# First attention of a two-layer adaLN kernel: negated scores, one product as the division, weight casts on ScalarE, a new order on four engines

## The chip, the cores and the metric

The kernel runs on one core of a Trainium2 chip. Five engines work side by side, each through its own list in order: TensorE (PE; its weight loads are PEld), VectorE (DVE), ScalarE (ACT), GpSimd (POOL) and SyncE (SP), which issues the DMAs. They wait for each other on semaphores. The metric is the device time of one execution in microseconds (us).

## The reference, cut to what matters

Two layers on x of shape (2, 512, 512), each an attention block and a feed-forward block behind an adaptive layer norm. All is float32. The change touches only the first layer's attention:

```python
q = (x @ wq).reshape(B, S, 32, 128)     # 32 query heads, 8 key/value heads
k = (x @ wk).reshape(B, S, 8, 128)
v = (x @ wv).reshape(B, S, 8, 128)
q, k = _rope(q, pos), _rope(k, pos)
scores = jnp.einsum('bqhgd,bshd->bhgqs', qg, k) * sm_scale   # 128 ** -0.5
allowed = (j <= i) & (j > i - 128)
attn = jax.nn.softmax(jnp.where(allowed, scores, neg), axis=-1)
out = jnp.einsum('bhgqs,bshd->bqhgd', attn, v).reshape(B, S, 32 * 128)
return out @ wo                          # then x = x + ga * out
```

## The kernel before, in words

Float32 products are made of three matmuls (`mm3`): each operand is split into a rounded high part (written as float32r by a copy) and a low remainder (operand minus high part), and high x high, high x low and low x high are added in PSUM.

The first attention goes over 8 key/value heads (`kv_head(n, last)`: head 0 by itself, heads 1 to 6 in a hardware loop, head 7 with `last`). A head has two halves, one for each batch element b, numbered half = 2n + b. A half has four slots, one for each block of 128 queries (qb = 0 to 3), numbered slot = 4 half + qb. In a slot four query heads are done together: `scores` into banks 0 and 1; `mask` on DVE (L1126), which scales, adds the window, and keeps each row's maximum, then L1138 negates the four maxima; `exps` on ACT (L812), with the row sums beside them; `normalise` on DVE (L1140), a reciprocal of 128x4 and four multiplications (L1147); `transposes` on PE (L1568); `weights_high` on ACT and `weights_low` on DVE (the split); `sum_values` on PE into bank 4; `out_high` and `out_low` (the split of its result); `project_out` on PE into bank 5; `gate_attention` on DVE; `add_attention` on POOL into x. A query sees only its own and the preceding block of keys, so slot 0 of a half is 128 wide and the others 256.

Between these stand the projections of the next half (`project`: Q0 to Q3, Vt, which is V's transpose) and of the one after it (K, V), into banks 6 and 7 by turns. `evacuate` on DVE (three instructions, L1122 to L1124) makes the rope terms, POOL adds them (L613), ACT rounds (L806), POOL makes the remainder (L616). The weights of head n + 1 are split within head n: `split_weights` and `split_wo` cast on DVE (L1100, L1105), POOL subtracts (L602, L606). SP reloads a staging tile when `w_split` and `wo_split` say that it was read.

There is no planner: the order on each engine is the order in which the lines of that engine's `kv_head` stand. Buffers are few. `probs` and `nmax` have two copies, by qb % 2; banks 0 to 5, `pT_hi`, `oT_hi` and `gated` one. `scores(slot)` waits until slot - 1 is masked, `transposes(slot)` until slot is divided and `pT_lo` of slot - 1 is made, `sum_values(slot)` until `oT_lo` of slot - 1 is made, `project_out(slot)` until slot - 1 is gated.

Of the kernel before, what the change touches and what calls it, by code (L numbers as in the profile page):

```python
# [55 lines left out]
def adaln_two_layers(nc, a, out):  # L56
# [7 lines left out]
    with ctx:  # L64
# [51 lines left out]
        rmax = sb0("rmax", [P, 2, GQ])  # L116
# [166 lines left out]
        scores0, rowmax0, masked0, exp0, rden0, probs0 = (sem(n) for n in ("scores0", "rowmax0", "masked0", "exp0", "rden0", "probs0"))  # L283
# [312 lines left out]
        def _(pool):  # L596
# [11 lines left out]
            def rope(half, name, b):  # L608

                r = 5 * half + ROPE_NO[name]  # L610
                i = (b + ROPE_NO[name]) % 2
                pool.wait_ge(proj_free, TURNS * half + TURN[name] + 1)
                pool.tensor_tensor(rope_a[:, i], rope_a[:, i], rope_b[:, i], ALU.add).then_inc(rope_sum, 1)  # L613
                pool.wait_ge(rope_hi, r + 1)
                hi, lo = (kT_hi[:, b], kT_lo[:, b]) if name == "K" else (qT_hi[b][:, ROPE_NO[name] - 1], qT_lo[b][:, ROPE_NO[name] - 1])
                pool.tensor_tensor(lo, rope_a[:, i], hi.bitcast(F32), ALU.subtract).then_inc(rope_split, 1)  # L616

# [142 lines left out]
        def _(act):  # L760
# [51 lines left out]
            def exps(slot, qb):  # L812
# [3 lines left out]
                for h in range(GQ):  # L816
                    e = act.activation(probs[:, i, h, c], probs[:, i, h, c], ACT.Exp, bias=nmax[:, i, h:h + 1], scale=1.0,  # L817
# [8 lines left out]

            def kv_head(n, last):
                for b in range(B):
                    half, slot, nb = 2 * n + b, 8 * n + 4 * b, 1 - b
                    more = not (last and b == 1)  # L830
                    weights_high(slot, 0)
                    exps(slot + 1, 1)
                    if isinstance(n, int) and n == 0 and b == 0:
                        gates(0, 0, gate_a0)
                    out_high(slot)
                    if more:
                        rope_high(half + 1, "Q0", nb)
                    weights_high(slot + 1, 1)
                    if more:
                        v_high(half + 1, nb)  # L840
                        rope_high(half + 1, "Q1", nb)
                    exps(slot + 2, 2)
                    out_high(slot + 1)
                    weights_high(slot + 2, 2)
                    if more:
                        rope_high(half + 1, "Q2", nb)
                    exps(slot + 3, 3)
                    out_high(slot + 2)
                    if more:
                        rope_high(half + 1, "Q3", nb)  # L850
                    weights_high(slot + 3, 3)
                    if not last:
                        rope_high(half + 2, "K", b)
                    out_high(slot + 3)
                    if more:
                        exps(slot + 4, 0)

# [160 lines left out]
        def _(dve):  # L1018
# [70 lines left out]
            def split_weights(n, tiles):  # L1089

                for m in tiles:
                    src = st_kv[:, m] if m < 2 else st_q[:, :, (m - 2) * HD:(m - 1) * HD]
                    if m < 2:
                        dve.wait_ge(kv_loaded, 32 * n + 32)
                    else:
                        dve.wait_ge(q_loaded, 16 * n + 16)
                    if not isinstance(n, int) or n > 0:
                        name = [k for k, v in W_TILE.items() if v == m][0]
                        dve.wait_ge(proj_done, TURNS * (2 * n - 1) + TURN[name] + 1)
# [26 lines left out]
            def mask(slot, qb):  # L1126
# [41 lines left out]
            def kv_head(n, last):  # L1168
                for b in range(B):
# [4 lines left out]
                    if b == 0:  # L1174
                        split_wo(n)
# [5 lines left out]
                    out_low(slot)  # L1181
# [811 lines left out]
```

## Time and profile before

| | us |
|---|---|
| median of 3 runs | 2474.5 (2472.98 to 2479.92) |
| profiled execution, its span | 2475.1 |
| PE busy | 2315.8 (94%) |
| DVE busy | 1807.3 (73%) |
| ACT busy | 1336.2 (54%) |
| POOL busy | 580.5 (23%) |

The span runs from the first to the last instruction of one profiled execution; no separate time of that execution is listed. Busy times of an engine are summed over its instructions; matmuls overlap, and their ends are modelled. "Idle before" in a row is the time in which the engine stood before those instructions, and behind the arrow is who ended it. The first attention takes roughly 70 to 835 us of the span, the first feed-forward block ends by about 915 us, the second attention by about 2400 us.

### The profile page before, as it was taken

Reading aid. Unit: us, or ns where it says so; the run is one execution under the profiler, and the core shown is the slowest. Engines: PE = TensorE matmul, PEld = TensorE weight load, DVE = VectorE, ACT = ScalarE, POOL = GpSimd, SP = SyncE. Lnnn points to the kernel's source line nnn. Section 1 sums busy time; section 2 is a strip of 40 time slices with the busy share of each in tenths; the row PEclk is TensorE's granted clock in tenths of the full one; section 3 lists DMA queues with packets and bytes.
Section 4 is the critical chain, followed back from the end, with each engine's and each line's share of the span. In section 5 each row is a group of like instructions: output and inputs, shape, how many; then the busy total and the mean of one; then the engine's idle time right before and its main releaser. Section 6 shows DMA issues by size and latency. Waiting matters only on the chain.

```text
span 2475.1 us, 41157 instructions
## 1 busy us (share of the span) xinstructions
PE 2315.8 (94%) x11084; PEld 1674.6 (68%) x11084; DVE 1807.3 (73%) x3372; ACT 1336.2 (54%) x2583; POOL 580.5 (23%) x428
## 2 busy tenths in 40 slices
PE   6898898998998788999999999999999999999988
PEld 4677777777776555666666666666666666666655
DVE  6788889888887465676676776776776766767856
ACT  2333333333333324776676766766766766766641
POOL 4355545455544041000000000000000000001432
PEclk9899999999999888999999999999999999999998
DMA  5101001001003204111111111111111111112330
GB/s 192 44 26 43 17 25 42 17 25 42 17 0 86 79 1 155 33 38 38 36 37 37 33 36 38 36 37 37 32 37 38 36 37 33 37 37 69 107 82 35
DMA packets 114848, 113.31 MB, mean 46 GB/s; under 512 B 28669, under 2 KB 71197, under 8 KB 114796
## 3 DMA queue, kind: packets, MB, share of 16 engines
q1 hardware_dynamic: 114796, 112.66, 15.4%
q8 instruction: 27, 0.44, 0.1%
q14 instruction: 25, 0.20, 0.0%
HBM read 93.20 MB, written 18.87 MB: 45 GB/s over the span
## 4 chain that ended last, share of the span: by engine, by line
PE 73%; DVE 15%; ACT 4%; issue 3%; DMA 1%; SPq 1%; POOL 1%; DVEq 0%; POOLq 0%; ACTq 0%
PE bank L1773 11%; PE bank L1786 10%; PE bank L1799 10%; PE bank L1787 9%; PE bank L1761 5%; PE bank L1759 5%; PE bank L1760 5%; PE bank L1485 4%; PE bank L1487 4%; PE bank L1486 4%; ACT probs L817 3%; DVE probs L1147 3%; DVE probs L1134 2%; DVE nmax L1138 2%; PE bank L1573 2%
## 5 line engine op out<-in xcount | busy, mean ns | idle before, releaser
L1334 DVE TENSOR_REDUCE mcol<-bank 128x1 fp32r<-128x512 f32 x1024 | 702.3, 690 | 393.3 <-PE bank L1773 386.5
L958 ACT ACTIVATE pT<-bank 128x512 f32<-128x512 f32 x1024 | 598.9, 599 | 368.4 <-PE bank L1787 340.8
L1773 PE MATMUL bank<-km,q 128*128 128x512 f32 x1024 | 434.8, 426 | 5.7 <-DVE mcol L1334 3.4
L1786 PE MATMUL bank<-q,k 128*128 128x512 f32 x1024 | 418.5, 409 | 6.6 <-DVE c_lo L1305 3.2
L1773 PEld LDWEIGHTS bank<-km,q 128*128 128x128 f32 x1024 | 316.8, 310 | 155.5 <-DVE mcol L1334 113.1
L1787 PE MATMUL bank<-q,k 128*128 128x512 f32 x1024 | 405.8, 396 | 0.0
L697 POOL TENSOR_TENSOR wr_lo<-wst,wr_hi 128x512 fp32r<-128x512 f32 x64 | 82.6, 1291 | 1267.1 <-DVE wr_hi L1293 1267.1
L1786 PEld LDWEIGHTS bank<-q,k 128*128 128x128 f32 x1024 | 195.7, 191 | 131.0 <-ACT pT L958 108.2
L1799 PE MATMUL bank<-pT,vp 128*32 128x512 f32 x2048 | 272.7, 605 | 0.7 <-ACT pT L958 0.7
L1787 PEld LDWEIGHTS bank<-q,k 128*128 128x128 f32 x1024 | 192.8, 188 | 37.8
L1761 PE MATMUL bank<-hT_hi,wr_lo 128*128 128x512 f32 x512 | 207.0, 404 | 0.0
L1759 PE MATMUL bank<-hT_hi,wr_hi 128*128 128x512 f32 x512 | 204.9, 400 | 2.1 <-DVE q L1315 1.2
L1760 PE MATMUL bank<-hT_lo,wr_hi 128*128 128x512 f32 x512 | 203.6, 398 | 0.0
L817 ACT ACTIVATE probs<-probs,nmax 128x256 f32<-128x256 f32 (+1 forms) x256 | 120.2, 471 | 133.5 <-DVE nmax L1138 133.5
L1485 PE MATMUL bank<-hT_hi,w_hi 128*128 128x512 f32 x384 | 156.4, 407 | 7.3 <-issue 4.4
L613 POOL TENSOR_TENSOR rope_a<-rope_a,rope_b 128x512 f32<-128x512 f32 x80 | 104.6, 1308 | 216.2 <-DVE rope_b L1124 216.2
L1487 PE MATMUL bank<-hT_hi,w_lo 128*128 128x512 f32 x384 | 154.9, 403 | 0.0
L1486 PE MATMUL bank<-hT_lo,w_hi 128*128 128x512 f32 x384 | 154.2, 402 | 0.0
L824 ACT ACTIVATE pT_hi<-bank 128x512 fp32r<-128x512 f32 x112 | 61.8, 596 | 160.5 <-PE bank L1573 160.5
L1573 PE MATMUL bank<-ident,probs 128*128 128x128 f32 x448 | 67.6, 295 | 75.0 <-DVE probs L1147 75.0
L1147 DVE TENSOR_SCALAR probs<-probs,rden 128x256 f32<-128x256 f32 (+1 forms) x256 | 128.3, 561 | 2.3
L1573 PEld LDWEIGHTS bank<-ident,probs 128*128 128x128 f32 x448 | 53.6, 150 | 98.0 <-DVE probs L1147 93.1
(266 smaller groups left out, 4056.8 us busy)
## 6 DMA issues: line engine op xcount, KB each, us to landing
wst<-in_L_attn_Wq_rope SPq DMA_DIRECT2D x64, 256.0 KB, 3.0
wm<-in_L_wmod SPq DMA_DIRECT2D x12, 1024.0 KB, 8.6
st_q<-in_L_attn_wq SPq DMA_DIRECT2D x8, 1024.0 KB, 7.4
st_wo<-in_L_attn_wo SPq DMA_DIRECT2D x8, 1024.0 KB, 5.2
km<-kc_d SPq DMA_DIRECT2D x256, 32.0 KB
q<-qc_d SPq DMA_DIRECT2D x256, 32.0 KB
k<-kc_d SPq DMA_DIRECT2D x256, 32.0 KB
o_d<-ost SPq DMA_DIRECT2D x512, 16.0 KB
```

What stands on the lines that cost most here:

```text
L958: act.activation(pT[:, s], bank[s % 4][:], ACT.Exp, scale=float((HD1 + ROPE) ** -0.5)).then_inc(exp1, 1)
L1334: dve.tensor_reduce(mcol[:, k % 2, i % 4, i // 4:i // 4 + 1], bank[4 + i % 2][:], AX.X, ALU.max, negate=True)\
L1485: pe.matmul(ps, lh_, rh, start=(i == 0), stop=False)
L1486: pe.matmul(ps, lh_, rl, start=False, stop=False)
L1487: e = pe.matmul(ps, ll, rh, start=False, stop=(i == n - 1))
L1759: pe.matmul(bank[6][:], wr_hi[:, par, kk], hT_hi[:, kk, at], start=(kk == 0), stop=False)
L1760: pe.matmul(bank[6][:], wr_hi[:, par, kk], hT_lo[:, kk, at], start=False, stop=False)
L1761: e = pe.matmul(bank[6][:], wr_lo[:, par, kk], hT_hi[:, kk, at], start=False, stop=(kk == KT - 1))
L1773: pe.matmul(bank[4 + i % 2][:], q2[:, k % 4, h, i % 4:S:4], km[:, b, h], start=True, stop=True).then_inc(max_mm, 1)
L1786: pe.matmul(bank[s % 4][:], k1[:, k % 2, t], q1[:, k % 4, h], start=True, stop=False)
L1787: pe.matmul(bank[s % 4][:], k2[:, k % 2, h, t], q2[:, k % 4, h], start=False, stop=True).then_inc(scores1, 1)
L1799: e = pe.matmul(bank[7][32 * j:32 * j + 32, :], vp[:, k % 2, kb, h], pT[:, s], start=(c == 0), stop=(c == 1))
```

## The change

It does five things, all within the first attention.
- `mask` scales by a negative number and keeps the minimum, so that `nmax` comes straight from it and L1138 with its wait is gone; `exps` takes scale -1.0.
- `normalise` multiplies all four heads in one `tensor_tensor`, the reciprocals broadcast along the row, in place of four `tensor_scalar`.
- The casts of `w_hi` (from head 1 on) and of `wo_hi` are made on ScalarE (`weights_high0`, `out_weights_high`) in place of VectorE.
- On PE, `scores(slot + 2)` and `scores(slot + 3)` stand ahead of `transposes(slot + 1)` and `transposes(slot + 2)`, Vt and Q2 earlier, K ahead of `transposes(slot + 3)`, and `sum_values(slot + 3)` ahead of the next half's scores.
- On DVE, ACT and POOL the lines are put in a new order; on POOL `rope` is cut into `rope_add` and `rope_low`, between which other work may stand.

The declarations of `rmax` and `rowmax0` go too, and VectorE's `split_weights` keeps only head 0's casts. On POOL `rope_add` is the old `rope` up to the sum, with its wait on `proj_free`; `rope_low` is the remainder, with its wait on `rope_hi`. The rest:

```diff
--- before.py
+++ after.py
@@ -641,25 +648,36 @@
             def kv_head(n, last):
...
                     half = 2 * n + b
+                    more = not (last and b == 1)
+                    split = b == 0 and not last
                     if not (isinstance(n, int) and n == 0 and b == 0):
                         add_attention(4 * half - 1, TB * (1 - b) + 3)
+                    if more:
+                        rope_add(half + 1, "Q0", 1 - b)
                     if b == 0:
                         split_wo(n)
-                    if not (last and b == 1):
-                        rope(half + 1, "Q0", 1 - b)
+                    if more:
+                        rope_low(half + 1, "Q0", 1 - b)
                         rope(half + 1, "Q1", 1 - b)
+                    if split:
+                        split_weights(n + 1, (0,))
                     add_attention(4 * half, TB * b)
-                    if b == 0 and not last:
-                        split_weights(n + 1, (0, 1))
-                    if not (last and b == 1):
+                    if more:
                         rope(half + 1, "Q2", 1 - b)
+                    if split:
+                        split_weights(n + 1, (1,))
+                    add_attention(4 * half + 1, TB * b + 1)
+                    if more:
                         rope(half + 1, "Q3", 1 - b)
-                    add_attention(4 * half + 1, TB * b + 1)
                     if not last:
-                        rope(half + 2, "K", b)
-                        if b == 0:
-                            split_weights(n + 1, (2, 3, 4, 5))
+                        rope_add(half + 2, "K", b)
+                    if split:
+                        split_weights(n + 1, (2,))
                     add_attention(4 * half + 2, TB * b + 2)
+                    if not last:
+                        rope_low(half + 2, "K", b)
+                    if split:
+                        split_weights(n + 1, (3, 4, 5))
                 if last:
@@ -814,7 +832,7 @@
                 for h in range(GQ):
-                    e = act.activation(probs[:, i, h, c], probs[:, i, h, c], ACT.Exp, bias=nmax[:, i, h:h + 1], scale=1.0,
+                    e = act.activation(probs[:, i, h, c], probs[:, i, h, c], ACT.Exp, bias=nmax[:, i, h:h + 1], scale=-1.0,
                                        accum_out=den[:, i, h:h + 1])
@@ -824,36 +842,68 @@
+            def weights_high0(n, m):
+
+                src = st_kv[:, m] if m < 2 else st_q[:, :, (m - 2) * HD:(m - 1) * HD]
+                if m < 2:
+                    act.wait_ge(kv_loaded, 32 * n + 32)
+                else:
+                    act.wait_ge(q_loaded, 16 * n + 16)
+                name = [k for k, v in W_TILE.items() if v == m][0]
+                act.wait_ge(proj_done, TURNS * (2 * n - 1) + TURN[name] + 1)
+                act.activation(w_hi[:, m], src, ACT.Copy).then_inc(w_hi_done, 1)
+
+            def out_weights_high(n):
+
+                act.wait_ge(wo_loaded, 16 * n + 16)
+                wait(act, wo_mm, 8 * n)
+                act.activation(wo_hi[:], st_wo[:], ACT.Copy).then_inc(wo_hi_done, 1)
+
             def kv_head(n, last):
...
                     more = not (last and b == 1)
+                    split = b == 0 and not last
                     weights_high(slot, 0)
...
                         gates(0, 0, gate_a0)
+                    if b == 0:
+                        out_weights_high(n)
                     out_high(slot)
+                    if split:
+                        weights_high0(n + 1, 0)
                     if more:
...
                         v_high(half + 1, nb)
+                    exps(slot + 2, 2)
+                    if more:
                         rope_high(half + 1, "Q1", nb)
-                    exps(slot + 2, 2)
                     out_high(slot + 1)
+                    if split:
+                        weights_high0(n + 1, 1)
                     weights_high(slot + 2, 2)
...
                     exps(slot + 3, 3)
+                    if split:
+                        weights_high0(n + 1, 2)
                     out_high(slot + 2)
+                    weights_high(slot + 3, 3)
                     if more:
                         rope_high(half + 1, "Q3", nb)
-                    weights_high(slot + 3, 3)
+                    out_high(slot + 3)
+                    if more:
+                        exps(slot + 4, 0)
+                    if split:
+                        weights_high0(n + 1, 3)
                     if not last:
                         rope_high(half + 2, "K", b)
-                    out_high(slot + 3)
-                    if more:
-                        exps(slot + 4, 0)
+                    if split:
+                        weights_high0(n + 1, 4)
+                        weights_high0(n + 1, 5)
             def out_high(slot):
@@ -1086,23 +1136,15 @@
-
-            def split_wo(n):
-                dve.wait_ge(wo_loaded, 16 * n + 16)
-                wait(dve, wo_mm, 8 * n)
-                dve.tensor_copy(wo_hi[:], st_wo[:]).then_inc(wo_hi_done, 1)
@@ -1131,11 +1173,9 @@
                     ps = bank[h // 2][:, (h % 2) * 2 * P:(h % 2 + 1) * 2 * P]
-                    e = dve.tensor_tensor_reduce(probs[:, i, h, c], ps[:, c], window[:, c], float(HD) ** -0.5, -3e38, ALU.add, ALU.max,
-                                                 rmax[:, i, h:h + 1])
-                e.then_inc(rowmax0, 1)
-                dve.wait_ge(rowmax0, slot + 1)
-                dve.tensor_scalar(nmax[:, i], rmax[:, i], -1.0, None, ALU.mult).then_inc(masked0, 1)
+                    e = dve.tensor_tensor_reduce(probs[:, i, h, c], ps[:, c], window[:, c], -(float(HD) ** -0.5), 3e38, ALU.add, ALU.min,
+                                                 nmax[:, i, h:h + 1])
+                e.then_inc(masked0, 1)
             def normalise(slot, qb):
@@ -1143,9 +1183,9 @@
                 dve.wait_ge(rden0, slot + 1)
-                for h in range(GQ):
-                    e = dve.tensor_scalar(probs[:, i, h, c], probs[:, i, h, c], rden[:, i, h:h + 1], None, ALU.mult)
-                e.then_inc(probs0, 1)
+                n = c.stop - c.start
+                dve.tensor_tensor(probs[:, i, :, c], probs[:, i, :, c], rden[:, i].unsqueeze(2).broadcast_to([P, GQ, n]), ALU.mult)\
+                   .then_inc(probs0, 1)
             def weights_low(slot, qb):
@@ -1171,20 +1211,16 @@
                         gate_attention(slot - 1, nb)
-                    if b == 0:
-                        split_wo(n)
                     weights_low(slot, 0)
...
                     normalise(slot + 1, 1)
+                    if more:
+                        evacuate(half + 1, "Q1", nb)
+                    mask(slot + 2, 2)
                     out_low(slot)
-                    if b == 0 and not last:
-                        split_weights(n + 1, (0, 1))
-                    if more:
-                        evacuate(half + 1, "Q1", nb)
                     weights_low(slot + 1, 1)
-                    mask(slot + 2, 2)
                     if more:
@@ -1192,8 +1228,8 @@
                         evacuate(half + 1, "Q2", nb)
+                    mask(slot + 3, 3)
                     weights_low(slot + 2, 2)
-                    mask(slot + 3, 3)
                     if more:
@@ -1204,8 +1240,6 @@
                         evacuate(half + 2, "K", b)
-                        if b == 0:
-                            split_weights(n + 1, (2, 3, 4, 5))
                     gate_attention(slot + 2, b)
@@ -1602,27 +1636,26 @@
                     sum_values(slot, half, b, 0)
                     if more:
                         project(half + 1, "Q1", nb, n + b)
+                        project(half + 1, "Vt", nb, n + b)
+                    scores(slot + 2, half, b, 2)
                     transposes(slot + 1, 1)
-                    scores(slot + 2, half, b, 2)
-                    if more:
-                        project(half + 1, "Vt", nb, n + b)
+                    if more:
+                        project(half + 1, "Q2", nb, n + b)
                     project_out(slot, n)
                     sum_values(slot + 1, half, b, 1)
-                    if more:
-                        project(half + 1, "Q2", nb, n + b)
+                    scores(slot + 3, half, b, 3)
                     transposes(slot + 2, 2)
-                    scores(slot + 3, half, b, 3)
                     if more:
                         project(half + 1, "Q3", nb, n + b)
                     project_out(slot + 1, n)
                     sum_values(slot + 2, half, b, 2)
-                    transposes(slot + 3, 3)
                     if not last:
                         project(half + 2, "K", b, n + 1)
+                    transposes(slot + 3, 3)
                     project_out(slot + 2, n)
+                    sum_values(slot + 3, half, b, 3)
                     if more:
                         scores(slot + 4, half + 1, nb, 0)
-                    sum_values(slot + 3, half, b, 3)
                     if not last:
                         project(half + 2, "V", b, n + 1)
                     project_out(slot + 3, n)
```

## Rows read from the trace of the kernel before

**Rows 1.** Page, part 1: busy us, share, instructions of each engine.

```profile
PE 2315.8 (94%) x11084; PEld 1674.6 (68%) x11084; DVE 1807.3 (73%) x3372; ACT 1336.2 (54%) x2583; POOL 580.5 (23%) x428
```

**Rows 2.** Stretches: length; PE, PEld, DVE, ACT, POOL busy; granted clock; DMA share, GB/s.

```profile
78.40:835.70 757.30, 677.13 (x3428) 560.57 (x3429) 635.63 (x1435) 274.97 (x771) 369.76 (x261) 0.97 0.10 29
...
1000.00:2300.00 1300.00, 1296.76 (x6170) 883.36 (x6172) 912.61 (x1492) 907.27 (x1545) 85.18 (x66) 1.00 0.14 38
...
276.60:372.40 95.80, 86.51 (x443) 71.81 (x443) 82.11 (x184) 35.02 (x98) 49.43 (x36) 0.98 0.09 27
```

**Rows 3.** Waits, 276.8 to 756.5 us (five heads): total us, times, longest.

```profile
PE bank L1573 <- DVE probs L1147: 45.8, 30, 3.9
```

**Rows 4.** Timeline of PE: start, duration, instruction, count, idle time before it.

```profile
297.61 1.09 PE L1573 MATMUL bank<-ident,probs 128*128 128x128 f32 x8 [1.40 <-DVE probs L1147]
298.45 0.36 PE L1485 MATMUL bank<-kT_hi,bq_hi 128*128 128x256 f32 x1
...
299.97 0.39 PE L1485 MATMUL bank<-hT_hi,w_hi 128*128 128x512 f32 x1
...
302.77 0.39 PE L1485 MATMUL bank<-wo_hi,oT_hi 128*128 128x512 f32 x1
...
305.53 0.40 PE L1485 MATMUL bank<-pT_hi,v_hi 128*128 128x512 f32 x1
...
314.45 0.23 PE L1485 MATMUL bank<-kT_hi,bq_hi 128*128 128x128 f32 x1
...
315.75 0.45 PE L1485 MATMUL bank<-pT_hi,v_hi 128*128 128x512 f32 x1
...
380.68 1.97 PE L1573 MATMUL bank<-ident,probs 128*128 128x128 f32 x8 [3.89 <-DVE probs L1147]
...
797.81 0.60 PE L1573 MATMUL bank<-ident,probs 128*128 128x128 f32 x4
...
835.05 0.39 PE L1485 MATMUL bank<-wo_hi,oT_hi 128*128 128x512 f32 x1
```

**Rows 5.** Timeline of DVE and POOL, the same columns.

```profile
276.81 3.73 DVE L1138 TENSOR_SCALAR nmax<-rmax 128x4 f32<-128x4 f32 x1
...
294.36 3.19 DVE L1147 TENSOR_SCALAR probs<-probs,rden 128x256 f32<-128x256 f32 x4
...
371.70 4.62 POOL L606 TENSOR_TENSOR wo_lo<-st_wo,wo_hi 128x2048 fp32r<-128x2048 f32 x1
372.60 3.75 DVE L1138 TENSOR_SCALAR nmax<-rmax 128x4 f32<-128x4 f32 x1
...
804.06 1.14 DVE L1147 TENSOR_SCALAR probs<-probs,rden 128x256 f32<-128x256 f32 x4
```

**Rows 6.** Groups by line and shape: busy us, mean ns; idle before.

```profile
L1147 DVE TENSOR_SCALAR probs<-probs,rden 128x256 f32<-128x256 f32 x192 | 97.5, 567 | 1.7
L1153 DVE TENSOR_TENSOR pT_lo<-bank,pT_hi 128x512 fp32r<-128x512 f32 x112 | 72.8, 686 | 27.7 <-ACT pT_hi L824 26.8
L1134 DVE CUSTOM_DVE_ANT_0 probs<-bank,window 128x256 f32<-128x256 f32 x192 | 69.6, 418 | 2.7 <-PE bank L1487 2.7
L1100 DVE CAST w_hi<-st_q 128x512 fp32r<-128x512 f32 x32 | 21.3, 723 | 0.2
L1086 DVE TENSOR_TENSOR hT_lo<-full,hT_hi 128x512 fp32r<-128x512 f32 x16 | 20.7, 1291 | 0.5
L1105 DVE CAST wo_hi<-st_wo 128x2048 fp32r<-128x2048 f32 x8 | 9.7, 1216 | 0.0
L1455 DVE TENSOR_TENSOR cmpe<-prob 128x1800 f32<-128x1800 f32 x1 | 2.0, 2026 | 0.0
L1469 DVE TENSOR_TENSOR lh_lo<-lh,lh_hi 128x512 fp32r<-128x512 f32 x2 | 1.4, 686 | 0.1
L806 ACT ACTIVATE bq_hi<-rope_a 128x512 fp32r<-128x512 f32 x64 | 40.3, 629 | 59.0 <-POOL rope_a L613 59.0
```

**Rows 7.** Chain of work that ended last, one piece: start, us.

```profile
339.76 2.09 ACT probs L817 x8
```

More of the change, by code:

```diff
@@ L115, in adaln_two_layers @@
         w_lo = sb0("w_lo", [P, NPROJ, KT, HD], F32R)
-        rmax = sb0("rmax", [P, 2, GQ])
         nmax = sb0("nmax", [P, 2, GQ])
@@ L282, in adaln_two_layers @@
         rope_sum, rope_hi, rope_split, v_hi_done = sem("rope_sum"), sem("rope_hi"), sem("rope_split"), sem("v_hi_done")
-        scores0, rowmax0, masked0, exp0, rden0, probs0 = (sem(n) for n in ("scores0", "rowmax0", "masked0", "exp0", "rden0", "probs0"))
+        scores0, masked0, exp0, rden0, probs0 = (sem(n) for n in ("scores0", "masked0", "exp0", "rden0", "probs0"))
         trans0, pT_hi_done, pT_split, pv0 = sem("trans0"), sem("pT_hi_done"), sem("pT_split"), sem("pv0")
@@ L606, in split_wo, with rope_add @@
                 pool.tensor_tensor(wo_lo[:], st_wo[:], wo_hi[:].bitcast(F32), ALU.subtract).then_inc(wo_split, 1)
-            def rope(half, name, b):
-                r = 5 * half + ROPE_NO[name]
+            def rope_add(half, name, b):
                 i = (b + ROPE_NO[name]) % 2
@@ L613, in rope, with rope_low @@
                 pool.tensor_tensor(rope_a[:, i], rope_a[:, i], rope_b[:, i], ALU.add).then_inc(rope_sum, 1)
+            def rope_low(half, name, b):
+                r = 5 * half + ROPE_NO[name]
+                i = (b + ROPE_NO[name]) % 2
                 pool.wait_ge(rope_hi, r + 1)
@@ L616, in rope @@
                 pool.tensor_tensor(lo, rope_a[:, i], hi.bitcast(F32), ALU.subtract).then_inc(rope_split, 1)
+            def rope(half, name, b):
+                rope_add(half, name, b)
+                rope_low(half, name, b)
             def add_attention(slot, tile):
@@ L847, in kv_head @@
                     exps(slot + 3, 3)
+                    if split:
+                        weights_high0(n + 1, 2)
                     out_high(slot + 2)
+                    weights_high(slot + 3, 3)
                     if more:
                         rope_high(half + 1, "Q3", nb)
-                    weights_high(slot + 3, 3)
-                    if not last:
-                        rope_high(half + 2, "K", b)
                     out_high(slot + 3)
@@ L856, in kv_head @@
                         exps(slot + 4, 0)
+                    if split:
+                        weights_high0(n + 1, 3)
+                    if not last:
+                        rope_high(half + 2, "K", b)
+                    if split:
+                        weights_high0(n + 1, 4)
+                        weights_high0(n + 1, 5)
             def out_high(slot):
@@ L1087, in norm_split, with split_weights @@
                                           ALU.subtract).then_inc(ln_lo, 1)
-            def split_weights(n, tiles):
+            def split_weights(tiles):
                 for m in tiles:
@@ L1093, in split_weights @@
                     if m < 2:
-                        dve.wait_ge(kv_loaded, 32 * n + 32)
+                        dve.wait_ge(kv_loaded, 32)
                     else:
[L1096 to L1099, printed above, removed]
+                        dve.wait_ge(q_loaded, 16)
                     dve.tensor_copy(w_hi[:, m], src).then_inc(w_hi_done, 1)
-            def split_wo(n):
-                dve.wait_ge(wo_loaded, 16 * n + 16)
-                wait(dve, wo_mm, 8 * n)
-                dve.tensor_copy(wo_hi[:], st_wo[:]).then_inc(wo_hi_done, 1)
             def evacuate(half, name, b):
@@ L1180, in kv_head @@
                     normalise(slot + 1, 1)
-                    out_low(slot)
-                    if b == 0 and not last:
-                        split_weights(n + 1, (0, 1))
                     if more:
                         evacuate(half + 1, "Q1", nb)
+                    mask(slot + 2, 2)
+                    out_low(slot)
                     weights_low(slot + 1, 1)
-                    mask(slot + 2, 2)
                     if more:
@@ L1224, in _ @@
             mod_cols(0, 0)
-            split_weights(0, (0, 1))
+            split_weights((0, 1))
             norm_split(0, 0)
-            split_weights(0, (2, 3))
+            split_weights((2, 3))
             norm_split(0, 1)
-            split_weights(0, (4, 5))
+            split_weights((4, 5))
             dve.wait_ge(rope_loaded, 48)
```

## The prediction

> **What bounds the kernel now.** I read the engine totals first: TensorE is busy 94% of the span and VectorE 73% [rows 1]. Then the stretches. The second attention runs TensorE at 1296.8 of 1300 us, granted clock 1.00; the change leaves it alone. The first attention is different: over the 757.3 us from its first to its last transposes and output product, TensorE is busy 677.1, VectorE 635.6, ScalarE 275.0, GpSimd 369.8, at clock 0.97, and one K/V head of 95.8 us has TensorE busy 86.5 [rows 2]. So some 9.3 us per head are idle. The waits say where: over five heads TensorE stands 45.8 us, 30 times, before the transposes of the weights (L1573), waiting for the division on VectorE (L1147) [rows 3]. That is 9.2 us a head, six waits, nearly all of the idle time. Other engines wait longer, but they aren't the bound. The reader is to see a latency chain rather than a full engine: scores, mask with maximum (DVE), exponentials (ACT), division (DVE), transposes (PE), with too little other work on TensorE's list between scores and transposes.
>
> **What a head costs TensorE without waits.** Start to start [rows 4]: eight transposes 0.84 us (297.61 to 298.45), scores of a 256-wide block 1.52, a projection 2.80, an output product 2.76, a single matmul of these 2.80 / 12 = 0.233, so the sum over values 6 x 0.233 = 1.40 (half for block 0), scores of block 0 1.30 (314.45 to 315.75). A half has six projections 16.80, V's four transposes 0.42, weights' transposes 0.42 + 3 x 0.84 = 2.94, scores 1.30 + 3 x 1.52 = 5.86, sums 0.70 + 3 x 1.40 = 4.90, output products 11.04: 41.96, and a head 83.9. The head takes 95.8 (372.60 - 276.81 [rows 5]), so 11.9 are lost: 9.2 of waits, 6 x 0.17 of pipeline drained, and about 1.7 after the longest wait: behind 3.89 us of idle the eight transposes took 1.97 instead of 1.09 [rows 4].
>
> **The change part by part.**
>
> *The negation goes.* L1138 is a 128x4 operation, yet at 372.60 it took 3.75 us: GpSimd had begun the 4.62 us wo_lo subtraction at 371.70 and VectorE stood until it ended [rows 5]. That is the longest wait of each head (the 3.89 us one). Taking the minimum of the negated scores costs what the maximum did: same operands, 418 ns [rows 6]. At twice that (the upper bound; below, no gain) a mask would take 1.4 us more, inside the cover worked out below. I take nothing.
>
> *The division.* Four L1147 instructions average 567 ns [rows 6]; undisturbed all four take 1.14 us (804.06), beside GpSimd 3.19 (294.36) [rows 5]. The new one is a product of two SBUF tensors, 1024 elements wide. The nearest rows are 686 ns for 512 (L1469) and 2026 for 1800, there with broadcast operands (L1455): 1.04 ns an element, so 686 + 512 x 1.04 = 1.22 us, and 0.69 for block 0. Undisturbed it is slightly slower than the four. Beside GpSimd the row for one such product is 1291 against 686 (L1086) [rows 6], so it waits as well, but once per slot where four instructions could each meet a GpSimd operation. Bounds: 1.22 to 1.22 + 1.3 (a GpSimd operation of 512); 1.22 + 4.6 if it met wo_lo. I take 1.22, plus 1.2 at the two places named below.
>
> The Trainium skill (SBUF — State Buffer, Who interferes with whom) says that a VectorE product with both inputs in SBUF has to wait out a GpSimd operation that reads SBUF, as the two-port modes do; and VectorE: DVE Perf Modes (Why tensor_tensor can't do 2×_2P or 4×) that such a product never gets the doubled rate which fp32 tensor_scalar has. Both speak against this edit and the trace agrees: 1.14 for the four fast ones, 1291 against 686 for the product. By them alone the edit gains nothing where GpSimd rests.
>
> *The casts.* Six of w_hi and one of wo_hi leave VectorE: 6 x 0.72 + 1.22 = 5.5 us a head [rows 6], and they stood in the division's queue. ScalarE casts 512 in 0.63 [rows 6], so six take 3.8; the 2048-wide one lies between 0.63 and 4 x 0.63 = 2.5, and since it is four times the length I take 2.2: 6 us a head on an engine 35.0 us busy of 95.8 [rows 2]. Each waits only for a projection that is long done where it stands. Behind them in line: out_high(slot) and rope_high Q0 in b = 0, neither due for 3 us. Hidden. SP reloads st_kv and st_wo after w_split and wo_split, which come 5 to 15 us later in the head, 40 us before the next use. Hidden too.
>
> *The order.* Before, between scores(slot+2) and transposes(slot+2) TensorE had Vt, an output product, a sum and Q2: 7.4 us, against a chain that took 7.8 or more. Now it has transposes(slot+1), Q2, the output product, a sum and scores(slot+3): 9.3 us. The clean chain is 0.2 + 1.45 (mask, four every 0.35) + 2.09 (exponentials [rows 7]) + 0.2 (reciprocal) + 1.22 = 5.2 us. I walked a half through with these durations, PE at 0 with transposes(slot,0), VectorE in its new order:
> - transposes(slot+1) are due at 10.1. Q0 is evacuated at 6.9, the division collides with GpSimd's rope sum begun at 7.0, ends 9.5. In time.
> - transposes(slot+2) are due at 19.4. VectorE must first gate output product(slot), which TensorE ends at 16.7; gated at 17.35, GpSimd's add starts at once and holds the division to 18.7, ends 20.0. **Late by 0.6.**
> - transposes(slot+3): due 30.0, division ends 27.7. Next half's transposes: due 42.0, division ends 40.9.
> - sum_values(slot+3) has 0.84 + 2.76 = 3.60 of cover, and two copies (1.09), two subtractions (1.29, [rows 6]: 686 each, overlapping) and TensorE's drain need about 3.6. Late by 0 to 0.2.
> - wo_lo: GpSimd runs it after the rope sum and the division, 9.5 to 14.1; project_out(slot) is due at 13.8. Late by 0.4, in b = 0.
> - The last rope remainder (Q3) comes at 34.3, scores of the next half are due at 35.0.
>
> VectorE's own work is 32.2 us a half, 77% of 42. It isn't the bound.
>
> Waits per head: 2 x 0.6 + 2 x 0.1 + 0.4 = 1.8, with drained pipelines some 2.2. A head then takes 86.1, 9.7 less.
>
> **The sum.** Heads 1 to 6: 6 x 9.7 = 58. Head 0: its first half still waits for the gates (not moved), I take 8. Head 7: b = 0 without the K and V projections, by the same walk 6 less than the 44.8 it takes; the last half, from 797.81 to the last output product near 835.7 [rows 4], has no projections to hide anything. There the chain itself counts: per block 0.7 less mask and, because scores(slot+2) and (slot+3) go ahead of the transposes, the chains overlap; by the walk 31.8 instead of 37.9, 6 less. Sum 58 + 8 + 12 = 78. The profiled span is 2475.1, 0.6 above the median of 2474.5; no other time of that execution is given, so I take the difference off the median: **2396 us**.
>
> **The rivals.**
> 1. *All waits go, the clock too* (chance 0.12). 83.9 a head: 6 x 11.9 + 10 for head 0 + 14 for head 7 = 95, so 2379. For it: the slacks above are my estimates. Against: two lates depend on GpSimd's add, which follows the gate each time.
> 2. *VectorE's in-order list keeps half the waits* (0.18). gate(slot) stands ahead of the division and out_low(slot+1) ahead of evacuate Q2; each late TensorE step comes back through them. With 5 to 7 us of waits a head (half of today's 11.9) the gain is 5.5 x 8 = 44: 2430. For it: six waits today by such queueing. Against: VectorE gains 20 us of room a head.
> 3. *GpSimd, not VectorE, gets through first between the rope sum and wo_lo* (0.05). The division(slot+1) would wait to 12.9, end at 14.1, against 10.1: 4.0 plus the slow restart 1.7, once a head: 5.7 x 8 = 46 less gain, 2442. Against: at 294.36 VectorE's instructions came in between back-to-back GpSimd ones.
> 4. *Slower: the clock* (0.03). The stage's granted clock is 0.97; TensorE's share would rise from 90 to 97%. If it were granted 0.85 in return, a head would be 86.1 x 0.97 / 0.85 = 98.3, and 8 x 2.5 = 20 us are lost: 2494. It decides from 0.87 down. Against: 1.00 at 99.8% busy in the second attention [rows 2].
> The rest (0.62) is the forecast, with 2386 to 2410 its own range.
>
> **How the numbers follow.** A difference of 0.3% (7 us) is about what a measurement tells here. Low end: rival 1 at 2379 with a little for the clock, 2375. High end: into rival 2, 2428; outside lie some 0.05 below and 0.12 above. Faster: 0.62 + 0.12 + 0.18 + 0.05, less 0.02 for what I did not see: 0.95. Slower 0.04, same 0.01.
>
> **What would show it.** L1138 gone and no VectorE instruction of 3.7 us in the stage; head period near 86 (right below 88, wrong above 91); TensorE's wait before L1573 from 9.2 to 1 to 2.5 us a head, the one left being that of block 2; VectorE near 64 of 86 us; L1147's successor at 1.2 or 2.5 us, once per slot; clock 0.98 or more. Wrong if the waits before L1573 stay above 4 us a head, if VectorE waits for ScalarE's casts, or if scores wait for the rope remainders.

## The result and the profile after

| | before | after |
|---|---|---|
| median, us | 2476.9 (2472.98 to 2479.92, 4 runs) | **2399.2** (2394.12 to 2402.55, 4 runs) |
| ratio, 95% interval | | **0.9685** (0.9668 to 0.9701) |
| span of the profiled execution | 2475.1 | 2398.4 |

The forecast was 2396, so the time fell by 3.1% where 3.2% was said. In part 1 of the page of after (busy us, share, instructions), against [rows 1], VectorE's busy time fell by 121.5 us and TensorE's, with the same number of matmuls, by 16.7:

```profile
PE 2299.1 (96%) x11084; PEld 1662.8 (69%) x11084; DVE 1685.8 (70%) x3066; ACT 1368.8 (57%) x2633; POOL 588.5 (25%) x428
```

The stretches of after, with the columns of [rows 2]. The first runs from the first transposes to the last output product of the first attention; before, it was 757.3 us long:

```profile
77.40:755.50 678.10, 657.65 (x3428) 548.39 (x3429) 514.15 (x1133) 307.64 (x821) 377.64 (x261) 1.00 0.10 33
755.50:2398.00 1642.50, 1588.83 (x7429) 1078.10 (x7427) 1130.13 (x1848) 1041.65 (x1777) 181.45 (x140) 0.98 0.16 47
```

The stretch is 79.2 us shorter, and the span 76.7: all of the gain is here. Its granted clock rose from 0.97 to 1.00, and TensorE's busy time fell by 19.5 us, a quarter of the gain. That is the clock: 677.1 x 0.97 / 1.00 is 657, and 657.65 was measured. Before, once a head, TensorE ran at its lower level (1.2 of 2.4 GHz) after standing 3.89 us [rows 4], as this stretch shows (columns of [rows 2]); it begins with the eight transposes that took 1.97 us and take 1.03 to 1.09 now:

```profile
380.70:383.60 2.90, 2.90 (x14) 2.90 (x15) 2.89 (x5) 0.92 (x2) 1.05 (x1) 0.51 0.14 54
```

Waits of TensorE over 276 to 700 us of after (4.9 heads), as in [rows 3]. Two kinds remain, both short:

```profile
PE bank L1519 <- DVE rope_b L1166: 5.2, 10, 0.6
PE bank L1607 <- DVE probs L1187: 2.0, 5, 0.4
```

L1607 is the old L1573, the transposes of the weights: from 9.2 us a head to 0.4. The other is new: the projection Q2 waits until VectorE has evacuated Q1 from the bank that it is to write. Groups of after in the first attention, by shape (busy us, mean ns, idle before), against [rows 6]:

```profile
L1187 DVE TENSOR_TENSOR probs<-probs,rden 128x1024 f32<-128x1024 f32 x48 | 83.0, 1730 | 1.7
L1176 DVE CUSTOM_DVE_ANT_0 probs<-bank,window 128x256 f32<-128x256 f32 x192 | 70.0, 421 | 4.8 <-PE bank L1521 3.9
L854 ACT ACTIVATE w_hi<-st_q 128x512 fp32r<-128x512 f32 x28 | 16.6, 617 | 0.0
L860 ACT ACTIVATE wo_hi<-st_wo 128x2048 fp32r<-128x2048 f32 x8 | 15.2, 1903 | 0.0
```

### The profile page after: what moved, and what is told of

It is laid out like the page before. It is cut to its first block, busy times and chain, and to the rows that moved or that the text cites. A ratio compares the mean times of both kernels' runs of the same rounds, so it can differ in the third digit from the quotient of the medians.

```text
span 2398.4 us, 40901 instructions
## 1 busy us (share of the span) xinstructions
PE 2299.1 (96%) x11084; PEld 1662.8 (69%) x11084; DVE 1685.8 (70%) x3066; ACT 1368.8 (57%) x2633; POOL 588.5 (25%) x428
## 4 chain that ended last, share of the span: by engine, by line
PE 86%; DVE 7%; issue 2%; DMA 1%; SPq 1%; POOL 1%; ACT 1%; POOLq 0%; DVEq 0%; ACTq 0%
PE bank L1806 11%; PE bank L1819 11%; PE bank L1832 10%; PE bank L1820 10%; PE bank L1519 8%; PE bank L1521 8%; PE bank L1520 8%; PE bank L1794 5%; PE bank L1792 5%; PE bank L1793 5%; PE bank L1607 1%; DVE probs L1187 1%; DMA wm<-in_L_wmod 1%; DVE rope_b L1166 1%; DVE rope_a L1164 1%
## 5 line engine op out<-in xcount | busy, mean ns | idle before, releaser
L1519 PE MATMUL bank<-hT_hi,w_hi 128*128 128x512 f32 x384 | 157.2, 409 | 14.5 <-DVE rope_b L1166 9.2
L1794 PEld LDWEIGHTS bank<-hT_hi,wr_lo 128*128 128x128 f32 x512 | 97.0, 189 | 23.6
L1792 PEld LDWEIGHTS bank<-hT_hi,wr_hi 128*128 128x128 f32 x512 | 97.2, 190 | 22.5 <-DVE q L1349 4.3
L1793 PEld LDWEIGHTS bank<-hT_lo,wr_hi 128*128 128x128 f32 x512 | 96.9, 189 | 21.7
```

The source lines that it names most:

```text
L1519: pe.matmul(ps, lh_, rh, start=(i == 0), stop=False)
L1792: pe.matmul(bank[6][:], wr_hi[:, par, kk], hT_hi[:, kk, at], start=(kk == 0), stop=False)
L1793: pe.matmul(bank[6][:], wr_hi[:, par, kk], hT_lo[:, kk, at], start=False, stop=False)
L1794: e = pe.matmul(bank[6][:], wr_lo[:, par, kk], hT_hi[:, kk, at], start=False, stop=(kk == KT - 1))
```

## The experiments

Ratios are to the kernel before, run beside each, with 95% intervals. Gains and losses in the text are differences of ratios times 2477 us: for a_ against the kernel before (ratio 1), for the others against after (0.9685) where nothing else is said. The labels that begin with a_ are the kernel before with one edit, u_ the kernel after with one edit taken back, d_ and v_ add waits on GpSimd. v_q0, v_both and v_wo were timed in 5 rounds, the others in 3.

| label | us | ratio |
|---|---|---|
| a_neg | 2445.4 | 0.9864 (0.9846 to 0.9882) |
| a_div | 2462.3 | 0.9936 (0.9913 to 0.9959) |
| a_cast | 2493.2 | 1.0055 (1.0037 to 1.0073) |
| a_order | 2486.5 | 1.0026 (1.0015 to 1.0036) |
| u_neg | 2407.1 | 0.9712 (0.9694 to 0.9730) |
| u_div | 2459.5 | 0.9935 (0.9915 to 0.9954) |
| u_cast | 2422.5 | 0.9770 (0.9750 to 0.9791) |
| u_order | 2447.6 | 0.9878 (0.9861 to 0.9894) |
| d_late | 2419.3 | 0.9763 (0.9746 to 0.9780) |
| v_q0 | 2398.6 | 0.9672 (0.9654 to 0.9691) |
| v_both | 2392.4 | 0.9657 (0.9642 to 0.9672) |
| v_wo | 2385.0 | 0.9631 (0.9615 to 0.9647) |

**One edit alone.** a_neg:

```diff
-                    e = dve.tensor_tensor_reduce(..., float(HD) ** -0.5, -3e38, ALU.add, ALU.max, rmax[:, i, h:h + 1])
-                e.then_inc(rowmax0, 1)
-                dve.wait_ge(rowmax0, slot + 1)
-                dve.tensor_scalar(nmax[:, i], rmax[:, i], -1.0, None, ALU.mult).then_inc(masked0, 1)
+                    e = dve.tensor_tensor_reduce(..., -(float(HD) ** -0.5), 3e38, ALU.add, ALU.min, nmax[:, i, h:h + 1])
+                e.then_inc(masked0, 1)
...                                                      # and exps with scale=-1.0
```

> The kernel before with the negation edit alone. Cover theory (TensorE waits because the chain scores to division is longer than the work placed between): every chain loses 0.2 to 0.7 us, six waits a head, and the division of slot 1 in b = 0 still meets the wo_lo subtraction which the negation met, so its wait goes from 3.9 to about 2. Some 5 us a head, 40 us in all. Load theory (what pays is VectorE's freed time, in proportion): 7.5 of the 20 us a head that the whole change frees, so 0.37 of 78, 29 us.

It gained 34 us, between the 40 of the one theory and the 29 of the other, and so decides neither. About half of it is clock: TensorE's busy time is 2299.2 us against 2315.8, its longest wait over 276 to 700 us is 2.3 us, and the granted clock of 200 to 700 us is 1.00 against 0.98. a_div:

```diff
-                for h in range(GQ):
-                    e = dve.tensor_scalar(probs[:, i, h, c], probs[:, i, h, c], rden[:, i, h:h + 1], None, ALU.mult)
-                e.then_inc(probs0, 1)
+                n = c.stop - c.start
+                dve.tensor_tensor(probs[:, i, :, c], probs[:, i, :, c], rden[:, i].unsqueeze(2).broadcast_to([P, GQ, n]), ALU.mult)\
+                   .then_inc(probs0, 1)
```

> The kernel before with the one broadcast product alone. Cover theory: undisturbed 1.22 against 1.14 us, one GpSimd operation in the way instead of up to two, so only the divisions that took 3.2 us gain (1.7 each, one of them ahead of a TensorE wait): 1 to 2 us a head, 8 to 15 us. Load theory: about 5 of 20 us a head, 20 us.

It gained 16 us, which again lies between the theories (8 to 15, and 20). a_cast, with the rest of the order as before, in short:

```diff
+                    if b == 0:
+                        out_weights_high(n)            # ScalarE, likewise weights_high0 for the six tiles
-                    if b == 0:
-                        split_wo(n)                    # VectorE, likewise split_weights(n + 1, ...)
```

> The kernel before with the casts on ScalarE alone. Cover theory: wo_hi is now cast behind the exponentials, so wo_lo starts behind the negation of slot 1 and the 3.75 us stall goes; the two w_hi casts leave the queue ahead of mask(slot + 2), 1.2 us. 5 us a head, 40 us, largely the same microseconds as a_neg. Load theory: 5.5 of 20 us, 21 us.

**It was slower, by 14 us**, where both theories had a gain, though VectorE is rid of 5.5 us of casts a head. Its timeline (start, duration, idle before) on VectorE, GpSimd and TensorE, one fence for each engine, shows why:

```profile
382.08 0.18 DVE L1166 RECIPROCAL rden<-den 128x4 f32<-128x4 f32 x1
382.29 5.39 DVE L1169 TENSOR_SCALAR probs<-probs,rden 128x256 f32<-128x256 f32 x4
```
```profile
382.90 4.64 POOL L606 TENSOR_TENSOR wo_lo<-st_wo,wo_hi 128x2048 fp32r<-128x2048 f32 x1 [5.54 <-ACT wo_hi L842]
```
```profile
387.74 1.11 PE L1589 MATMUL bank<-ident,probs 128*128 128x128 f32 x4 [4.41 <-DVE probs L1169]
```

The wo_lo subtraction, which met the negation before [rows 5], now starts within the four instructions of a division, which take 5.39 us instead of 1.14, and TensorE stands 4.41. TensorE's busy time rose as well, from 2315.8 us to 2325.8, and the granted clock of 200 to 700 us is 0.97 against 0.98: part of the loss is clock. a_order, the new order of all engines with the casts on VectorE, the maximum and four instructions kept:

```diff
                     scores(slot + 2)
+                    scores(slot + 3)                   # PE; and so on as in the change
                     transposes(slot + 2)
```

> The kernel before with the new order on all engines, the negation, four divisions and the casts left on VectorE. Cover theory: 9.3 us between scores and transposes instead of 7.4, so four or five of the six waits of 0.8 to 1.4 us go and the one behind wo_lo stays above 2: 5 to 6 us a head, 45 us. Load theory: VectorE still has 82 us a head to do, no time freed, gain below 15 us.

Slower too, by 6 us, where the cover theory had 45 us of gain: a division took 7.35 us there (378.29), with wo_lo (4.59) at 379.37.

**One edit taken back.** u_neg, the diff of a_neg reversed:

> The changed kernel with the negation put back. Cover theory: wo_lo now starts well behind it, so it costs 0.2 to 0.7 us per slot, most of it inside the slack: 1 to 2 us a head, 2399 plus 8 to 15. Rival (the negation itself was what cost): it meets GpSimd operations as before, 5 us a head, plus 40.

It lost 7 us, where the one theory had 8 to 15 and the rival 40: none of its 64 negations takes more than 0.96 us, since wo_lo no longer meets them. u_div, the diff of a_div reversed:

> The changed kernel with four tensor_scalar divisions put back. Each now alternates with GpSimd: contended slots take 1.9 to 3.2 us against 2.2 to 2.3. Cover theory: 0 to 1 us a head, within 8 us of 2399 either way. Rival (fewer acquisitions of the shared ports is what pays): over 2 us a head, plus 20.

**It lost 62 us.** The cover theory (8 us at most) failed. The rival, that it pays to have fewer instructions which can meet a GpSimd operation, held, but its 2 us a head were far too few: it is nearly 8. The timeline of u_div, VectorE, GpSimd and TensorE:

```profile
363.60 0.18 DVE L1184 RECIPROCAL rden<-den 128x4 f32<-128x4 f32 x1
363.81 7.35 DVE L1187 TENSOR_SCALAR probs<-probs,rden 128x256 f32<-128x256 f32 x4
371.08 0.68 DVE L1164 TENSOR_TENSOR rope_a<-bank,rope_cos 128x512 f32<-128x512 f32 x1
```
```profile
363.64 1.30 POOL L611 TENSOR_TENSOR rope_a<-rope_a,rope_b 128x512 f32<-128x512 f32 x1 [4.84 <-DVE rope_b L1166]
364.89 4.59 POOL L605 TENSOR_TENSOR wo_lo<-st_wo,wo_hi 128x2048 fp32r<-128x2048 f32 x1
369.44 1.30 POOL L619 TENSOR_TENSOR bq_lo<-rope_a,bq_hi 128x512 fp32r<-128x512 f32 x1
```
```profile
371.22 1.42 PE L1607 MATMUL bank<-ident,probs 128*128 128x128 f32 x8 [4.52 <-DVE probs L1187]
```

Three GpSimd operations, back to back, sum to 7.19 us. VectorE's four instructions, taken apart, start at 363.81, 365.01 and 369.55 and take 1.28, 4.62 and 1.35 us, the fourth 0.28: each of the first three waits out one GpSimd operation. All executions of that line in u_div and in after (count, then min, median and max in ns, first and last start):

```profile
L1187 DVE TENSOR_SCALAR probs<-probs,rden x256: 274/346/4629, 73.8 to 804.0; 128x256 f32<-128x256 f32 x96, 128x128 f32<-128x128 f32 x32
```
```profile
L1187 DVE TENSOR_TENSOR probs<-probs,rden x64: 691/1338/2331, 76.6 to 743.1; 128x1024 f32<-128x1024 f32 x48, 128x512 f32<-128x512 f32 x16
```

The one product in after starts among the same operations and waits for the first alone. Its timeline at the same place of the next head, VectorE and GpSimd:

```profile
345.03 2.21 DVE L1187 TENSOR_TENSOR probs<-probs,rden 128x1024 f32<-128x1024 f32 x1
```
```profile
344.87 1.29 POOL L611 TENSOR_TENSOR rope_a<-rope_a,rope_b 128x512 f32<-128x512 f32 x1 [4.79 <-DVE rope_b L1166]
346.12 5.58 POOL L605 TENSOR_TENSOR wo_lo<-st_wo,wo_hi 128x2048 fp32r<-128x2048 f32 x1
```

Now it is wo_lo that takes about 1 us longer (5.58 against 4.62 [rows 5]); the product is over 1.12 us after it starts. That only shows two things side by side; d_late tests it. It is u_div, four instructions kept, with wo_lo held until that division is done:

```diff
                     if b == 0:
+                        pool.wait_ge(probs0, 4 * half + 2)
                         split_wo(n)
```

> As u_div (four tensor_scalar divisions in the changed kernel), but GpSimd begins wo_lo only when the division of slot 1 is done. If the 60 us of u_div are wo_lo (4.6 us) taking the shared ports between two of the four instructions, 4.5 us of wait and a slow restart once a head go: 2459 minus 40 to 50, 2409 to 2419. If they are a sum of many small collisions, minus 10 at most.

It won back 43 of the 62 us with nothing but the start of one GpSimd operation; the expectation had 40 to 50. The longest of its division instructions takes 1.40 us, against 4.63. TensorE's waits before the transposes over 276 to 700 us, in u_div and then in d_late:

```profile
PE bank L1607 <- DVE probs L1187: 30.4, 19, 4.5
```
```profile
PE bank L1608 <- DVE probs L1188: 14.5, 15, 1.6
```

These 14.5 us, against 2.0 in after, go with the other 19: shorter GpSimd operations still come between the four. No run tests that part by itself.

Not all of the 62 us are waits. TensorE's busy time is 2318.9 us in u_div, 2303.4 in d_late and 2299.1 in after, so some 20 of the 62 and 15 of the 43 lie in slower matmuls, most of them by the clock. Behind the 4.52 us that it stands at 366.7 to 371.2, TensorE is soon at its lower level, and a matmul of a projection starts every 0.43 us there instead of every 0.23 [rows 4]; u_div, columns of [rows 2]:

```profile
372.20:378.20 6.00, 5.34 (x15) 3.88 (x14) 4.81 (x14) 4.17 (x12) 2.11 (x2) 0.50 0.36 140
```

u_cast, the diff of a_cast reversed, the new order otherwise kept:

> The changed kernel with the casts back on VectorE, at their old places. They add 1.2 us ahead of weights_low(slot) in b = 0, 1.2 ahead of weights_low(slot + 1), 2.5 ahead of gate(slot + 2), and bring wo_lo forward onto the division of slot 1. Cover theory: 3 to 4 us a head, 2399 plus 25 to 32. Load theory: 5.5 us a head of VectorE's 20, plus 21, hard to tell apart here.

It lost 21 us, the figure of the load theory and near the 25 of the other; it can't tell them apart. A new wait stands in its list for 276 to 700 us, 1.9 us a head, and VectorE's timeline has four casts of w_hi ahead of oT_lo:

```profile
PE bank L1503 <- DVE oT_lo L1176: 9.5, 5, 1.9
```
```profile
385.11 3.62 DVE L1120 CAST w_hi<-st_q 128x512 fp32r<-128x512 f32 x4
```

u_order, the three edits in the old order:

> The changed kernel with the old order on all engines; negation, product and casts as changed. Cover theory: 7.4 us of cover against a chain of 5.2 to 6.5 undisturbed, so half of the waits stay: 3 to 5 us a head, 2399 plus 25 to 40. Load theory: all of VectorE's time is freed, so plus 0 to 8 us.

It lost 48 us, where the load theory had 8 at most and the cover theory 25 to 40: the transposes wait 17.9 us, 23 times, over 276 to 700 us, and products behind them 6.0 for pT_lo and 5.8 for wo_lo.

**A faster kernel.** The waits of after come from divisions that a GpSimd operation held up (2.22 and 2.33 us instead of 1.22). v_q0 holds back the rope sum, v_both the gated add too:

```diff
                     if more:
+                        pool.wait_ge(probs0, 4 * half + 2)   # v_q0 and v_both
                         rope_add(half + 1, "Q0", 1 - b)
...
+                    pool.wait_ge(probs0, 4 * half + 3)       # v_both
                     add_attention(4 * half, TB * b)
```

> The changed kernel; GpSimd begins the rope sum of Q0 only when the division of slot 1 is done. The collision that holds the division to 2.2 us goes, the evacuation of Q1 ends 1 us earlier, and TensorE's wait before Q2 (0.49 and 0.58 us a head, each with 0.17 of drained pipeline) goes: 1.4 us a head, 2399 minus 11 = 2388. Rival (GpSimd's delay comes back through wo_lo or the rope remainders): no change or slower.

> As v_q0, and GpSimd adds the first block of a half into x only when the division of slot 2 is done. The wait of 0.40 us before transposes(slot + 2), once a head, goes too: 2 us a head against the changed kernel, 2399 minus 16 = 2383, which is about 84 us a head. Rival as for v_q0.

v_q0 moved nothing that can be told (3 us, within the intervals), as its rival said: the waits before Q2 went, and wo_lo, started later, became a wait in their place. v_both is 7 us ahead of after, with intervals that just overlap, where 16 were expected. Its waits of TensorE, 276 to 700 us (those marked issue have no cause in the profile):

```profile
PE bank L1521 <- POOL wo_lo L605: 3.0, 4, 0.8
PE bank L1521 <- issue: 0.6, 1, 0.6
```

v_wo is v_both with wo_lo ahead of the rope sum, and with ScalarE's rounding of Q0 moved behind the exponentials of slot + 2; against v_both:

```diff
-                    if more:
-                        pool.wait_ge(probs0, 4 * half + 2)
-                        rope_add(half + 1, "Q0", 1 - b)
+                    pool.wait_ge(probs0, 4 * half + 2)
                     if b == 0:
                         split_wo(n)
                     if more:
+                        rope_add(half + 1, "Q0", 1 - b)
+                    if more:
                         rope_low(half + 1, "Q0", 1 - b)
...
-                    if more:
-                        rope_high(half + 1, "Q0", nb)        # ScalarE
...
                     exps(slot + 2, 2)
                     if more:
+                        rope_high(half + 1, "Q0", nb)
                         rope_high(half + 1, "Q1", nb)
```

> The kernel after with GpSimd starting neither wo_lo nor the gated add before the division that it would hold up, wo_lo now ahead of the rope sum of Q0 in its list, and ScalarE's rope_high of Q0 moved behind the exponentials of slot+2 (next to that of Q1). Against v_both (2392.4) this should remove the one wait that is left there each head: TensorE stood 0.77 us ahead of the output product of the slot, for wo_lo, with 0.17 us of drained pipeline: 0.94 x 8 = 7.5 us. Theory (wo_lo is late only because it stands behind a rope sum of 1.3 us): about 2385, the wait for wo_lo gone, 84 us a head. Rival 1: the rope sum of Q0 now comes after 4.6 us of wo_lo, and VectorE's remainder of Q0 comes late for the next half's scores, or stands in VectorE's list ahead of something due: a new wait of 0.5 us or more a head, 2390 to 2396. Rival 2: the exponentials keep ScalarE and nothing changes: 2392.

**2385.0 us, 3.7% below before**, as its theory said: 7 us ahead of v_both, again with intervals that just overlap, and 13 ahead of after, clear of noise. Which of its two moves does it, no run tells. Its one wait in the five heads, and its stretch:

```profile
PE bank L1608 <- DVE probs L1188: 0.6, 1, 0.6
```
```profile
77.00:742.00 665.00, 653.61 (x3428) 549.11 (x3429) 497.68 (x1136) 304.58 (x821) 363.80 (x261) 0.99 0.11 33
```

A head takes 83.7 us (wo_lo starts at 259.1 and 426.5, two heads apart). That is about the 83.9 that the prediction worked out for TensorE without a wait: this way of gaining is used up.

## Why the prediction was right, and where it was not

- **The floor and the losses.** The forecast had 83.9 us a head without waits, and v_wo measures 83.7. It had 11.9 us a head lost before, nearly all with the wait for the division, and of them 9.7 to be won. After takes 85.95 a head (wo_lo starts at 260.19, 346.12, 432.09), where 86.1 was forecast. The stretch fell by 79.2 us, the sum said 78. By the starts of wo_lo, heads 1 to 6 took 576.1 us before and 515.6 after: 60.5 of the 79.2, where 58 was forecast, and 18.7 for heads 0 and 7, where 20 was.
- **The restart.** The 1.7 us a head behind the longest wait were put in the sum without a cause. The rows show it: granted clock 0.51 behind that wait, and 1.00 over the first attention of after.
- **Negation.** Right: the mask with minimum takes 421 ns against 418, and no operation of 128x4 is caught behind wo_lo (the 64 reciprocals take 166 to 180 ns). a_neg gives the most of the four alone, 34 us.
- **The division: the cost right, the reason too small.** 1.22 was forecast undisturbed, 1.22 + 1.3 beside a GpSimd operation; the trace has 1.22 (408.57) and 2.33 (398.69). But the text took the four instructions' handicap to be that "each could meet a GpSimd operation" and priced it nowhere. It is the largest single term: with the other three edits made, four instructions cost 62 us more than one product. The two rules of the Trainium skill quoted there (SBUF — State Buffer, Who interferes with whom; VectorE: DVE Perf Modes, Why tensor_tensor can't do 2×_2P or 4×) hold in these rows: the product waits out GpSimd (2.33 us), and it isn't faster by itself (1.22 against 1.14). "By them alone the edit gains nothing where GpSimd rests" was true and beside the point, as GpSimd doesn't rest there.
- **Casts.** ScalarE's take 0.62 (0.63 forecast) and 1.90 for wo_hi (2.2 forecast), hidden as said. Rival 3 named the operation that matters, wo_lo between the rope sum and the rest, but had it hit the one product. None of the 64 products of after is hit: the longest takes 2.33 us, one GpSimd operation and itself. It hits the four instructions, as u_div shows.
- **The walk: its total right, its places not.** Forecast were late transposes of block 2 by 0.6 in each half, wo_lo late by 0.4, oT_lo by 0.1. Measured per head: 0.40 before the transposes, once; nothing for wo_lo or oT_lo; and two waits of 0.50 and 0.59 before Q2, forecast nowhere. The step that fails is "the division collides with GpSimd's rope sum begun at 7.0, ends 9.5. In time.": that asks who waits for the division, not who waits for what stands behind it on VectorE. These rows of after, VectorE and then TensorE, show Q1's evacuation pushed back by the division and Q2's projection behind it:

```profile
387.67 2.22 DVE L1187 TENSOR_TENSOR probs<-probs,rden 128x1024 f32<-128x1024 f32 x1
389.80 0.68 DVE L1164 TENSOR_TENSOR rope_a<-bank,rope_cos 128x512 f32<-128x512 f32 x1
390.50 0.69 DVE L1165 TENSOR_TENSOR rope_b<-bank,rope_sin 64x512 f32<-64x512 f32 x1
391.20 0.68 DVE L1166 TENSOR_TENSOR rope_b<-bank,rope_sin 64x512 f32<-64x512 f32 x1
```
```profile
392.02 0.49 PE L1519 MATMUL bank<-hT_hi,w_hi 128*128 128x512 f32 x1 [0.50 <-DVE rope_b L1166]
401.08 1.09 PE L1607 MATMUL bank<-ident,probs 128*128 128x128 f32 x8 [0.40 <-DVE probs L1187]
```

  Waits sum to 1.5 us a head and 1.8 were forecast. That they agree is partly luck, since most of them stand at places that the forecast passed as in time. The late Q2 also hides wo_lo: it ended at 351.70, and the output product began at 352.28, behind a Q2 that was 0.59 late; without that it would have been due at 351.69. v_q0, where wo_lo starts later, has the wait.
- **The rivals.** All waits gone (2379) is what v_wo comes near by other means. That VectorE's list keeps half the waits (2430) is nearest to what u_order (2447.6) and u_cast (2422.5) show, with the order or the casts put back, and not to after. The clock went up, not down.
- **What was not asked.** The forecast walked through all the edits together and put no price on each by itself. Alone they measure -34, -16, +14 and +6, together -30; all four give -78. In a_cast and a_order the operation of 4.6 us moves onto four short instructions; with the one product in place the casts and the order pay 21 and 48 us. Without it they cost: u_div, which is a_neg with the casts and the order, stands at 0.9935 and a_neg at 0.9864, 18 us apart. That VectorE's freed time is what brings the gain is refuted: a_cast frees 5.5 us a head and is slower, u_div gives VectorE nearly the same work (1.14 us a division undisturbed, for 1.22) and loses 62 us.

## What to carry to other kernels

Where GpSimd runs long SBUF operations, count VectorE's instructions on the critical chain and not only their time: here each was one chance to stand for a whole GpSimd operation, so that one long instruction beat four fast ones, and the long GpSimd operation was best started right behind the chain's VectorE step. Read TensorE's busy time beside its waits: here a long wait cost more than its own length, as the clock fell behind it. When an edit lengthens one instruction, follow each instruction behind it in that engine's list to its own waiter. Measure edits that free an engine together with those that fix the order: alone, two of the four looked harmful here.

## What the runs showed of the hardware

- VectorE and GpSimd took turns, an instruction at a time, where both had SBUF operations waiting (u_div): four tensor_scalar, 1.14 us undisturbed, took 7.35 us around GpSimd operations of 1.30, 4.59 and 1.30. A 128x4 operation is caught as a 1024-wide one is (3.75 us [rows 5]). GpSimd is held likewise: wo_lo takes 5.58 us when it starts beside a product, 4.61 in v_wo, where it starts behind one. VectorE's rope terms, which read one operand from PSUM, weren't held: at 347.17 to 349.24 in after they take 0.68 to 0.69 us each while wo_lo runs.
- The VectorE product of 1024 elements in a row takes 1.22 us with a broadcast operand, as the prediction's line through 686 ns for 512 and 2026 for 1800 had it.
- ScalarE's cast of 128x2048 takes 1.90 us, less than four casts of 512 at 0.617.
- TensorE's granted clock was 0.51 over 380.7 to 383.6 us of before, behind 3.89 us of idle, and 0.50 over 372.2 to 378.2 us of u_div, behind 4.52. A long wait isn't the only thing that goes with it: in u_cast, whose longest wait over 276 to 700 us is 1.9 us, the granted clock is 0.79 over 300 to 308 us. What decides it, no run here shows.
